# The three middle layers of a Fourier-operator chunk: written out in line instead of looped over, on four engines

## The reference

```python
x = coords @ fc0_w + fc0_b
x = jnp.transpose(x, (0, 3, 1, 2))
for sw, cw, cb in ((sw0, cw0, cb0), (sw1, cw1, cb1), (sw2, cw2, cb2), (sw3, cw3, cb3)):
    x1 = _spectral_conv(x, sw)          # rfft2, 20x20 modes mixed over channels, irfft2
    x2 = jnp.einsum('bchw,oc->bohw', x, cw) + cb[None, :, None, None]
    x = _gelu(x1 + x2)
x = jnp.transpose(x, (0, 2, 3, 1))
x = _gelu(x @ fc1_w + fc1_b)
return (x @ fc2_w + fc2_b)[..., 0]
```

## Time and profile before

| | us |
|---|---|
| median of 3 runs | 6175.48 |
| lowest and highest of them | 6164.15, 6176.18 |
| the profiled execution | 6138.44 |
| its span, first to last instruction | 6135.5 |
| busy: PE / PEld / DVE / ACT / POOL | 5481.0 / 4115.8 / 2832.0 / 2673.2 / 1103.5 |
| TensorE clock granted, mean share | 0.952 |

### The profile page before, as it was taken

How to read it: one execution, slowest core, us unless ns; L and a number is a source line. 1 busy time by engine, 2 the same in 40 slices (tenths; PEclk the granted TensorE clock), 3 DMA queues, 4 the chain that set the end, 5 groups by cost and what they waited for, 6 DMA issues and landing times. The chain is left out here.

```text
span 6135.5 us, 273892 instructions
## 1 busy us (share of the span) xinstructions
PE 5481.0 (89%) x119157; PEld 4115.8 (67%) x119157; DVE 2832.0 (46%) x4407; ACT 2673.2 (44%) x4998; POOL 1103.5 (18%) x1045
## 2 busy tenths in 40 slices
PE   8999999999899989989988998999999788888888
PEld 6776777678767776877677767776777443434343
DVE  4443444344434443444344434443444474848484
ACT  3335333533353335333533353335334564747473
POOL 4220322032202221222222222212221000000000
PEclk9999999999999999999999999999999798989898
DMA  2111111111111120111012101110110100000000
GB/s 35 14 15 15 20 14 14 17 18 14 14 18 17 14 25 9 15 20 19 10 14 25 14 10 23 16 15 12 20 16 4 22 1 8 1 8 1 4 1 4
DMA packets 442829, 85.51 MB, mean 14 GB/s; under 512 B 437336, under 2 KB 437608, under 8 KB 441544
## 3 DMA queue, kind: packets, MB, share of 16 engines
q1 hardware_dynamic: 439624, 67.23, 8.8%
q10 hardware_dynamic: 2048, 0.53, 0.0%
HBM read 63.51 MB, written 4.23 MB: 11 GB/s over the span
## 5 line engine op out<-in xcount | busy, mean ns | idle before, releaser
L218 POOL COPY x_T<-x_X 128x512 f32<-128x512 f32 x1024 | 1074.4, 1101 | 3565.4 <-ACTq L810 3386.6
L805 ACT ACTIVATE x_X<-ga 128x512 f32<-128x512 f32 x1280 | 751.3, 597 | 1098.7 <-PE ga L469 906.6
L658 DVE COPY x_X<-ev 128x512 f32<-128x512 f32 x640 | 438.3, 688 | 847.8 <-PE ev L488 778.3
L469 PEld LDWEIGHTS ga<-pw_rhs,x_X 64*64 64x64 f32 x32768 | 593.8, 135 | 279.7 <-issue 278.9
L658 DVE COPY V<-ev 104x512 f32<-104x512 f32 x608 | 411.2, 689 | 602.9 <-PE ev L435 444.8
L500 PEld LDWEIGHTS ev<-dft_consts,x_T 128*64 128x64 f32 x16384 | 578.7, 137 | 42.3 <-issue 41.9
L500 PE MATMUL ev<-dft_consts,x_T 128*64 128x80 f32 x16384 | 599.7, 234 | 4.3 <-POOL x_T L218 3.4
L469 PE MATMUL ga<-pw_rhs,x_X 64*64 64x64 f32 x32768 | 585.5, 218 | 5.0 <-issue 4.3
L461 PE MATMUL ga<-V,inv_w 40*64 40x512 f32 x4096 | 549.7, 604 | 29.6 <-ACT V L773 27.9
L658 DVE COPY Y<-ev 128x400 f32<-128x400 f32 (+1 forms) x768 | 462.8, 603 | 211.9 <-PE ev L500 167.5
L658 DVE COPY D<-ev 128x512 f32<-128x512 f32 x576 | 362.1, 684 | 330.7 <-PE ev L407 328.3
(11 more groups left out here) (210 smaller groups left out, 8216.4 us busy)
## 6 DMA issues: line engine op xcount, KB each, us to landing
mix_w<-in_sw SPq DMA_DIRECT2D x128, 400.0 KB
coords<-in_coords SPq DMA_DIRECT2D x66, 96.0 KB, 2.1
maps<-Y SPq DMA_DIRECT2D x128, 16.0 KB
raw<-maps SPq DMA_DIRECT2D x8, 256.0 KB, 3.5
out<-out_t SPq DMA_DIRECT2D x8, 256.0 KB, 3.5
w<-in_w SPq DMA_DIRECT2D x3, 512.0 KB, 6.9
dft_consts<-in_dft ACTq DMA_DIRECT2D x1, 336.0 KB
fc_rhs<-in_fc_w SPq DMA_DIRECT2D x16, 0.4 KB
```

The costliest lines, as they stand in the source:

```text
L218: pool.tensor_copy(x_T[:, :, H * bc + h0:H * bc + h0 + 16].rearrange("p c (s n) -> p c s n", n=2), blocks.rearrange("p (s a n c) -> p a c ...
L469: last = pe.matmul(ps[HALF * bp:HALF * bp + HALF, HALF * s:HALF * s + HALF], x_X[r:r + HALF, g, col:col + HALF], pw_rhs[r:r + HALF, :], st ...
L658: dve.tensor_copy(dst, src).then_inc(ev_taken, 1)
L805: x_new = act.activation(blocks.rearrange("p (s a n) -> p s a n", s=8, a=2)[:, :, bc, :], ga[n % N_GA][:, :].rearrange("p (s n) -> p s n", ...
```

## The change

The hardware loop over the layers becomes a Python loop. The four engines' code for a chunk then holds "mid" three times, each with its layer as a constant. The loop over the chunks stays, so the counts still depend on the chunk's register. SP's code and `token_program` stay as they are.

```diff
             def chunk_phases(chunk):
                 ev_c, ga_c = chunk * EV_CHUNK, chunk * GA_CHUNK
                 run("first", chunk, ev_c, ga_c, None)
-                with eng.Fori(0, LAYERS - 1) as layer:
-                    run("mid", chunk, ev_c + layer * EV_MID + EV_FIRST, ga_c + layer * GA_MID + GA_FIRST, layer)
+                for layer in range(LAYERS - 1):
+                    run("mid", chunk, ev_c + (layer * EV_MID + EV_FIRST), ga_c + (layer * GA_MID + GA_FIRST), layer)
                 run("last", chunk, ev_c + (EV_FIRST + (LAYERS - 1) * EV_MID), ga_c + (GA_FIRST + (LAYERS - 1) * GA_MID), LAYERS - 1)
```

## The result

Each kernel now has five runs, the three of the kernel before that stand above among them: the kernel before has a median of 6169.23 us (6155.99 to 6176.18), the changed kernel 6122.23 us (6108.84 to 6141.47). The ratio is 0.9935 with an interval of 0.9918 to 0.9952. The change makes the kernel faster by 0.65%, or 47 us by the medians.

What follows compares the result with a forecast made beforehand. TensorE (PE) was taken to bound the kernel. The branch's -19.6 us and the clock's -4 us, other terms 0, gave -23.6 us, from a median of 6175.5 to 6151.9 us, range 6132 to 6172 us.

Steps and rivals of the forecast that it cites:

- The branch: At turn_d(0), 16 passages over PE's layer-loop branch take 3.38 us each, 2.16 without it: 19.6 us gained.
- The clock behind the gap: From turn_d(0) to line 461, shorter idleness may spare TensorE clock falls: 4 us gained, ends 0 and 7.9.
- the eight that I had held up as the pattern: Passages from third layer to "last", no taken branch: 2.16 us gaps, then 12.90 us each to line 461, three in 11.44.
- Code no longer held: DVE, ACT and POOL would fetch the second and third layer each time: 0 us, at most 20.9 from layer 1.
- The straight path costs it as many packets as the loop: PE's code, fetched over q8 in both layers compared, 28 and 29 packets, would need as many without the loop: no added cost.
- 7.6 us ahead of the branch: Within the mix, the remaining difference between the 16 and eight passages; the branch can't have caused it, so taken as 0.
- Small edits: Constants replacing the register spare a few register instructions, at the loop's head and lines 388 and 667: 0 us, within 1.
- From the profile to the median: The gain, priced on the profiled execution of 6138.44 us, was carried over to the runs' median of 6175.48 us.
- The first: At turn_d(0) the gap stays, or its instruction fetch moves into straight code: gain 0 to 2 us, about 6174; chance 0.05.
- the second: Fetches of DVE, ACT and POOL cost up to 20.9 us, leaving 0 to 12 gained, 6163 to 6175; chance 0.10.
- the third: Late fetches stall ACT and DVE mid-layer, costing 41.6 us: net 18 us slower, 6193.5; chance 0.05.
- The fourth: All passages come to look like the eight without a taken branch, clock included: 27 to 35 us gained, 6140 to 6148; chance 0.25.

Runs made afterwards that it cites:

- place 79: Kernel before, loops kept, filler laying PE's chunk loop at its natural place 79 in a block of 256 instructions: 6176.02 us, ratio 1.0001.
- ACT only: Kernel before with the three middle layers written out on ACT alone, the other engines keeping their loop: 6145.36 us, ratio 0.9985.
- DVE and POOL only: Kernel before with the three middle layers written out on DVE and POOL alone, PE and ACT keeping their loops: 6138.54 us, ratio 0.9985.
- PE only: Kernel before with the three middle layers written out on PE alone, the other engines keeping their loop: 6108.83 us, ratio 0.9932.
- series 2: Second set of four kernels, on its own chip with its own runs of the kernel before (6168.36 us); the changed kernel, unedited, took 6133.02 us there, ratio 0.9943.
- place 181: Kernel before, loops kept, PE's chunk code moved 102 instructions later, its loop head at place 181 of a 256-instruction block: 6128.33 us, ratio 0.9934.
- place 233: Kernel before, loops kept, PE's chunk code moved 102 instructions earlier, its loop head at place 233 of a 256-instruction block: 6173.96 us, ratio 1.0016.

## Why the prediction was wrong in size

Profiles cut alike, sums in us of the 32 stretches of each kind, of the 24 from line 461 to the next mix within a chunk ("bodies"), of the tokens, and of all the rest. "Layout before" are four profiles with the kernel before's PE code (before, place 79, ACT only, DVE and POOL only), "layout after" three with the changed kernel's (twice the changed kernel, PE only); each is a mean, with its ends:

| | mix | gap | to line 461 | bodies | tokens | rest |
|---|---|---|---|---|---|---|
| layout before | 361.8 (358.8 to 365.4) | 89.3 (88.5 to 90.0) | 437.8 (429.4 to 447.1) | 2472.5 (2463.7 to 2495.0) | 1311.4 (1300.7 to 1317.2) | 1476.4 |
| layout after | 345.4 (341.1 to 350.2) | 67.4 (67.3 to 67.5) | 434.3 (431.7 to 439.1) | 2484.2 (2469.6 to 2493.2) | 1307.6 (1304.5 to 1311.6) | 1477.6 |
| difference | -16.4 | -22.0 | -3.5 | +11.7 | -3.8 | +1.2 |

That is -33 us for these profiled executions. Clear of the scatter are the gap and the mix, and so is the sum of the first three columns: 879.7 to 898.5 us before, 840.1 to 856.6 after, 41.8 less. The bodies and the tokens show no difference.

**The branch, -19.6 us: right, place and size.** The 16 gaps went from 54.14 to 33.43 us, 20.7 us less; the copy of DVE is late next, 2.09 us, as its row said. The run with lengthened gaps is the proof that this idle time costs at least its own length.

**The clock behind the gap, -4 us: the step that failed.** I priced the clock from `turn_d(0)` to line 461 alone, at 4 us with 7.9 as its end, and set all that lies in the mix to zero. By half of the time at half clock its part is 17.9 us with PE written out and 26.8 us for the changed kernel in series 2; even at the half of that which the runs' own scatter suggests it is 9 to 13 us. It came where I had not looked: PE's busy time in the mixes fell by 15.1 us, and to line 461 there is no difference clear of the scatter. The 16 stretches fell from 214.26 to 210.40 us, by 3.9 us, as forecast, but in the one pair of profiles, and that is luck: the eight that I had held up as the pattern rose from 103.19 to 115.28 us, and not one of them ran in 11.44 us again. Of the clock's part the gap's length is some 7 us, by the run that lengthened it, 3 more than my 4.

**Code no longer held, 0 us: right.** q14 went from 147 to 241 packets, and neither ACT's nor DVE's and POOL's copies cost anything (0.9985 each). The bound of 20.9 us from layer 1 was no bound of fetches.

**"The straight path costs it as many packets as the loop": right in count, and 0 us was too little.** There are 987 packets on q8 against 1010, but what a packet costs isn't fixed. It depends on where its boundary falls in PE's work, and writing the loop out moves the second and the third copy, "last" and the tokens. In the earlier trace rows I had 7.6 us ahead of the branch before my eyes and set them to zero, because the branch can't cause them. It doesn't; but I should have asked what can change a mix, and the "issue" rows of line 381, 70.1 us, would have told. What the shorter mixes are worth to the whole is less than their 16 us: at the end of the third copy, which lost no branch there but was moved, the eight mixes are 9 us shorter, but from the mix to line 461 the eight take 208.1 us instead of 209.8, because the stretch behind them is slower by as much. The term could not have been priced without running it, as the places of the new copies are in no row; it could only have widened the range, on both sides, for moving the code alone gave anything from 0.9934 to 1.0016.

**Small edits, 0 us: right in sum, incomplete in kind.** 40 table loads of ACT went that I had not seen coming, although shows one. They are worth at most 0.3%.

**From the profile to the median.** The two profiled executions differ by 6138.44 - 6113.5 = 24.9 us, close to my 23.6, and this is luck: the kernel before had been profiled in an execution 31 us below its median of 6169.23, the changed one 9 us below its own.

**The rivals.** The first and the second fell with the gap and with DVE and POOL's run; the third with the list of waits, where no such stalls of ACT or DVE came up in the layers. The fourth had nearly the size, 27 to 35 us, but its reason, passages that all come to look like the eight, is refuted by the eight themselves. Its size too fell short of the 47 us of the first comparison.

**What stays open.** Why a given place spares TensorE time at its lower level I can't derive: place 181 saves 26 us of half the half-clock time and place 233 saves 2, with mixes of 328.5 and 332.6 us. Nor is it shown what the 6 to 18 us are that lie beyond the gap's 29 (35 us measured in series 2, 47 in the first comparison). The place of the copies is the candidate, since it moves the mixes and since place 181 by itself gains 0.66%; but the kernel with lengthened gaps, whose copies lie within 8 to 16 instructions of the changed kernel's, has mixes of 356.6 us at a clock of 0.914 and takes 879.3 us from the mix to line 461, as the kernel before does. So the gap's length and the place may act on the clock together, and no run here separates them.

## What to carry to other kernels

A gap on the bounding engine is worth what is left of it when the next late thing is counted, and that can be read beforehand from a place of the same trace without the obstacle. But an edit that moves that engine's code is also a draw of new code places, worth between 0.7% less and 0.2% more time here; before a gain of that order is credited to its reason, move the unchanged kernel's code alone and see what that does. "Issue" stops at a fixed distance of instructions in the densest matmul stretch are the sign that a kernel is open to this. And a sum over stretches of one pair of profiles needs a second profile of the same code beside it: here such sums differed by 30 us between two executions of one layout.

## What the runs showed of the hardware

**Code fetch is not hidden in dense work.** PE stops at block boundaries about 256 instructions apart, for 0.3 to 2.2 us, when its matmuls are short, and goes on 1.1 to 1.6 us after the end of a packet of 16.4 KB on its instruction queue; moving the code by 102 instructions, from place 79 to 181, took 0.66% off the time, with nothing else changed. The Trainium skill, "Runtime: NRT & Kernel Launch", section "Instruction fetch mechanics", says that code comes in blocks of 16 KiB, 256 instructions, with which the packets and the distance of the stops agree. It also says that crossing a boundary is mostly hidden; in these mixes it isn't, and here the measurement decides.

**A taken branch on PE has a length that depends on the place,** 4.7 us at the median of the 16 taken ones at place 233, and up to 5.0 us, where two packets come one after the other. In the kernel before it is 3.5 us, at place 79, the same to within 8 instructions, 3.8 us, and at place 181 3.8 us too, so only 233 stands apart. A long one delays `turn_d(0)` in full (PE in order of time at place 233):

```profile
838.79 1.11 PE L409 MATMUL ev<-dft_consts,S 128*128 128x128 f32 x4 [4.81 <-issue]
```

**A branch hint moves the wait more than it removes it:** 1.75 us instead of 3.47 us at the median where the branch is taken, and a stop of 1.6 to 2.8 us each time it is not. With one exit for every two jumps back that was a loss.

**Table loads hang on the loop.** At lines 787 and 805 ACT loaded a table 56 times with the loop and 16 times without, 1.283 us each.
